# A grouped expert feed-forward kernel: the first block of each expert at a fixed address, and work moved between engines and queues

## The reference

```
h = gelu(einsum('bsh,bhi->bsi', x, Wi[expert]) + bi[expert])     # (32, 64, 1024)
o = einsum('bsi,bih->bsh', h, Wo[expert]) + bo[expert]
r = o + x
y = (r - mean(r)) * rsqrt(var(r) + 1e-12)
out = y * gamma[expert] + beta[expert]                            # (32, 64, 256), float32
```

## Time and profile before

| | |
|---|---|
| median of 3 runs | 142.51 us (141.81 to 144.18) |
| profiled execution, its own time | 141.87 us |
| its span, first to last instruction | 140.1 us |
| mean granted TensorE clock | 0.963 of full |
| DMA traffic | 29.78 MB, mean 212 GB/s |
| blocks of 4 samples | 9 |

### The profile page before, as it was taken

How to read it: one execution, slowest core, us unless ns; L and a number is a source line. 1 busy time by engine, 2 the same in 40 slices (tenths; PEclk the granted TensorE clock), 3 DMA queues, 4 the chain that set the end, 5 groups by cost and what they waited for, 6 DMA issues and landing times.

```text
span 140.1 us, 2511 instructions
## 1 busy us (share of the span) xinstructions
PE 116.3 (83%) x838; PEld 109.3 (78%) x838; DVE 100.0 (71%) x202; ACT 73.2 (52%) x135; POOL 74.4 (53%) x84
## 2 busy tenths in 40 slices
PE   0599901999899989989998998999899979978800
PEld 0498701999799979979997997999799879968700
DVE  3300079257978997897899799889979958676650
ACT  4002397377466738756673876576387743550000
POOL 3050270402767666576857658586839845543460
PEclk9999995599999999999999999999999999999995
DMA  4899988993199559919954991796380230101111
GB/s 107 308 290 393 395 276 315 411 392 122 37 328 402 178 147 391 396 40 306 373 221 136 389 401 57 264 384 256 80 336 4 62 104 0 37 7 42 37 37 37
DMA packets 11009, 29.78 MB, mean 212 GB/s; under 512 B 1644, under 2 KB 6252, under 8 KB 8812
## 3 DMA queue, kind: packets, MB, share of 16 engines
q1 hardware_dynamic: 8540, 22.59, 43.1%
q0 software_dynamic: 1728, 4.72, 10.6%
q10 hardware_dynamic: 720, 2.23, 4.8%
HBM read 27.17 MB, written 2.36 MB: 211 GB/s over the span
## 4 chain that ended last, share of the span: by engine, by line
PE 34%; DVE 27%; ACT 14%; issue 12%; DMA 8%; SPq 1%; POOLq 1%; POOL 1%; DVEq 0%; ACTq 0%
PE preact L618 7%; DMA wi_in<-w_in 6%; ACT wi_hi L381 6%; PE preact L592 6%; PE preact L591 6%; PE sums_ps L642 4%; DVE h_lo L508 4%; PE sums_ps L591 4%; PE sums_ps L592 4%; DVE wi_lo L484 4%; ACT h_hi L410 4%; DVE xT_r L501 4%; ACT preact L401 4%; DVE stats L517 3%; PE sums_ps L639 2%
## 5 line engine op out<-in xcount | busy, mean ns | idle before, releaser
L618 PE MATMUL preact<-xT_r,wi_lo 128*128 128x256 f32 x128 | 38.9, 304 | 9.7 <-DVE xT_r L501 9.7
L401 ACT ACTIVATE preact<-preact,params 128x256 f32<-128x256 f32 x54 | 22.0, 445 | 40.5 <-PE preact L592 29.5
L591 PE MATMUL preact<-xT_r,wi_hi 128*128 128x256 f32 x128 | 36.5, 285 | 0.0
L592 PE MATMUL preact<-xT_r,wi_hi 128*128 128x256 f32 x128 | 36.4, 284 | 0.0
L508 DVE TENSOR_TENSOR h_lo<-preact,h_hi 128x512 fp32r<-128x512 f32 x27 | 18.6, 690 | 24.0 <-ACT h_hi L410 23.3
L618 PEld LDWEIGHTS preact<-xT_r,wi_lo 128*128 128x128 f32 x128 | 24.6, 193 | 13.1 <-DVE xT_r L501 12.9
L642 PE MATMUL sums_ps<-wo_r,h_lo 128*128 128x256 f32 x108 | 31.0, 287 | 1.9 <-issue 1.2
L591 PE MATMUL sums_ps<-wo_r,h_hi 128*128 128x256 f32 x108 | 30.7, 284 | 0.0
L592 PE MATMUL sums_ps<-wo_r,h_hi 128*128 128x256 f32 x108 | 30.5, 282 | 0.0
L233 POOL DMA_INDIRECT y_rows<-xs,row_of x18 | 25.0, 1388 | 9.8 <-DVE xs L530 7.2
L329 POOL TENSOR_TENSOR rstd<-var_eps,minus_half 128x1 f32<-128x1 f32 x18 | 13.1, 727 | 28.7 <-DVE var_eps L521 28.7
(11 more groups left out here) (55 smaller groups left out, 130.0 us busy)
## 6 DMA issues: line engine op xcount, KB each, us to landing
wi_in<-w_in SPq DMA_DIRECT2D x8, 1024.0 KB, 7.1
wo_in<-w_out SPq DMA_DIRECT2D x8, 1024.0 KB, 5.9
params<-vectors SPq DMA_DIRECT2D x9, 388.0 KB, 7.2
xT_in<-x_columns SPq DMA_DIRECT2D x34, 64.0 KB
wi_in<-w_in ACTq DMA_DIRECT2D x2, 512.0 KB, 5.4
wo_in<-w_out ACTq DMA_DIRECT2D x1, 1024.0 KB, 9.2
xs<-x_rows,row_of POOLq DMA_INDIRECT x18, 4.4
y_rows<-xs,row_of POOLq DMA_INDIRECT x18, 5.2
```

The costliest lines, as they stand in the source:

```text
L401: done = nc.scalar.activation(to, pre, ACT.Gelu, bias=params[:, t % PAR_RING, 3 * H + c:3 * H + c + 1])
L591: nc.tensor.matmul(columns, weight, parts[:, 0, :], start=False, stop=False)
L592: return nc.tensor.matmul(columns, weight, parts[:, 1, :], start=False, stop=stop)
L618: nc.tensor.matmul(columns, wi_lo[:, t % 2, c, k, :], xT_r[:, t % 2, k, 0, :], start=(k == 0), stop=False)
```

## The change

**Blocks.** Blocks 0 to 7 now belong to experts 0 to 7, whatever the draw: block `e` has the first four samples of expert `e` (empty rows if there are fewer, also when there are none). Only later fours of an expert are placed by the sort, from block 8 on. `MIN_BLOCKS` stays 8, `MAX_BLOCKS` goes from 14 to 15. With the draw above both kernels run 9 blocks, 3 to 8 of them in another order of experts. The samples of blocks 0 to 7 no longer need the count of the other experts' blocks, so they leave the sort after one matmul; the rest of the table follows. `expert(eng, t)` is a constant for `t < 8`.

**Loads at the start.** Block 1's `wi_in` is issued by ACT right behind block 0's `xT_in` and ahead of `wo_in` of block 0. SP issues `xT_in` of block 1, then its `params` and `wo_in`, without waiting for `table_ready`. `wi_in` has 3 slots, `params` 4.

**Engines.** The high part of `xT_r` goes from DVE (`split_x`) to ACT (`x_high`); DVE keeps the low part (`x_low`) and does it earlier in the iteration. Adding epsilon goes from DVE to GpSimd, ahead of the root. The stores go from GpSimd (one indirect transfer of 128 rows for half a block) to SP (two direct transfers of one sample each, 64 rows); the very last sample is stored by ACT. Six warm-up matmuls run on TensorE before the sort's first matmul and three behind the second, none next to block 0.

```diff
 def load_wi(eng, t, e):
-    if t == 2:
+    if t == WI_RING:
         eng.wait_ge(preact_ready, BANKS)
-    elif t > 2:
-        eng.wait_ge(wi_lo_done, wi_count(t - 2, 1))
+    elif t > WI_RING:
+        eng.wait_ge(wi_lo_done, wi_count(t - WI_RING, 1))
...
-def store(pool, t, tile):
-    pool.wait_ge(y_ready, 2 * t + tile + 1)
-    pool.indirect_dma_start(out.rearrange("o s h -> (o s) h"), rows_of(t, tile), xs[:, t % X_RING, tile, :],
-                            None).then_inc(stored[t % X_RING], 16)
+def store(eng, t, tile, first=0, count=2):
+    rows = samples(eng, t, 2 * tile + first, count)
+    eng.wait_ge(y_ready, 2 * t + tile + 1)
+    for j, b in enumerate(rows, 2 * tile + first):
+        eng.dma_start(out[bass.ds(b, 1), :, :].rearrange("o s h -> (o s) h"), slot(t, j)).then_inc(
+            stored[t % X_RING], 16)
...
 # SyncE
     load_xT(sp, 0, 0, 2)
-    sp.wait_ge(table_ready, 1)
-    second = expert(sp, 1)
-    load_wi(sp, 1, second)
     load_xT(sp, 1)
-    load_params(sp, 1, second)
-    load_wo(sp, 1, second)
+    load_params(sp, 1, 1)
+    load_wo(sp, 1, 1)
     def iteration(t, ahead):
         if ahead:
             e = expert(sp, t + 2)
             load_xT(sp, t + 2)
             load_wi(sp, t + 2, e)
             load_params(sp, t + 2, e)
+        if t >= 2:
+            store(sp, t - 2, 1)
+        if t >= 1:
+            store(sp, t - 1, 0)
+        if ahead:
             load_wo(sp, t + 2, e)
 # GpSimd
 def root(t, tile):
-    pool.wait_ge(var_ready, 2 * t + tile + 1)
+    at = 2 * t + tile + 1
+    pool.wait_ge(mean_done, at)
+    nc.gpsimd.tensor_scalar(var_eps[:, tile:tile + 1], meanvar[:, tile, 1:2], LN_EPS, None, ALU.add).then_inc(
+        var_ready, 1)
+    pool.wait_ge(var_ready, at)
     nc.gpsimd.tensor_tensor(rstd[:, tile:tile + 1], var_eps[:, tile:tile + 1], minus_half[:, :], ...
...
 # ScalarE
     load_xT(act, 0, 2, 2)
+    load_wi(act, 1, 1)
     load_wo(act, 0, 0)
...
+def x_high(t):
+    act.wait_ge(xT_loaded[t % 2], 4 * loads_of(t, 2))
+    if t >= 3:
+        act.wait_ge(preact_ready, BANKS * (t - 2) + BANKS)
+    nc.scalar.activation(x_part(t, 0), x_got(t), ACT.Copy).then_inc(x_hi_done, 1)
...
     h_high(t, 0)
+    if has_next:
+        x_high(t + 1)
     gelu(t, 1)
 # TensorE, start
+    pe.wait_ge(fills_done, 2)
+    warm_up(WARM_UP)
     pe.wait_ge(sort_step, 3)
+    nc.tensor.matmul(tab_ps[0:1, 0:FIRST], one, placed[:, 0:FIRST], start=True, stop=True).then_inc(permuted, 1)
...
-    for _ in range(WARM_UP):
-        nc.tensor.matmul(preact[:, 0, 0:P], warm[:, :], warm[:, :], start=True, stop=True)
```

More of the change, by code:

```diff
@@ L174, in expert @@
         def expert(eng, t):
-            return nc.values_load(table[0:1, T_EXPERT + t:T_EXPERT + t + 1], engines=[eng.engine], min_val=0, max_val=E - 1,
+            if t < E:
+                return t
+            at = T_EXPERT + t - E
+            return nc.values_load(table[0:1, at:at + 1], engines=[eng.engine], min_val=0, max_val=E - 1,
                                   skip_runtime_bounds_check_because="the sort places experts 0 to E - 1")
@@ L179, in row, with x_got, x_part @@
             return params[:, t % PAR_RING, which * H:(which + 1) * H]
+        def x_got(t):
+            return xT_in[:, t % 2, :, :, :].rearrange("p j k s -> p k j s")
+        def x_part(t, part):
+            return xT_r[:, t % 2, :, part, :].rearrange("p k (j s) -> p k j s", j=QUAD)
         def slot(t, j):
@@ L343, in iteration @@
                 if t >= 1:
-                    store(pool, t - 1, 0)
+                    root(t - 1, 0)
             def end(t):
@@ L449, in _ @@
             dve.wait_ge(idx_loaded, 16)
             chain(nc.vector.tensor_copy(key[:, :], idx_i[:, :]))
-            dve.wait_ge(const_step, 3)
-            chain(nc.vector.scalar_tensor_tensor(same[:, :], key[:, 0:ALL], key[:, ALL:ALL + 1], before[:, :],
-                                                 ALU.is_equal, ALU.mult, accum_out=rank[:, :]))
+            own = key[:, B:B + 1]
+            dve.wait_ge(const_step, 4)
+            nc.vector.scalar_tensor_tensor(same[:, :], key[:, 0:B], own, before[:, :], ALU.is_equal, ALU.mult,
+                                           accum_out=rank[:, :])
@@ L462, in _ @@
-            dve.wait_ge(const_step, 6)
-            chain(nc.vector.scalar_tensor_tensor(placed[:, :], slot_iota[:, :], slot_of[0:B, 0:1], sample_less[:, :],
-                                                 ALU.is_equal, ALU.mult))
+            chain(nc.vector.tensor_scalar(after[:, :], key[:, 0:B], own, None, ALU.is_gt))
+            dve.wait_ge(permuted, 1)
+            nc.vector.tensor_tensor(table[:, 0:FIRST], tab_ps[0:1, 0:FIRST], table_base[:, 0:FIRST], ALU.add).then_inc(
+                samples_ready, 1)
```

225 lines of the change are left out of this document (116 added, 109 removed).

## The result

The changed kernel takes 134.69 us (median of 4, 134.53 to 135.04) where the kernel before takes 142.91 in the same comparison: 0.945 of the time, 95% interval 0.939 to 0.952. It is faster, as forecast, but by 5.5% and not by 10%: the forecast was 128.5 and its range ended at 133.5. Timed again later it took 133.58 (133.14 to 134.55), 0.935 [0.932, 0.939]. So medians of one kernel differ by about 1 us between comparisons, and the miss is 5 to 6 us. The medians are of all executions, while the ratios leave out those that fell in a slower state of the chip (some 2 to 3 us longer), and e4 and e5, which kept too few others, have no ratio.

The account below looks back on a forecast made before the run. Between blocks DVE's written order was taken as the bound, TensorE behind it. 140.1 - 5.7 - 5.6 - 0.8 - 1.9 = 126.1 us of span, 128.5 as the median; range 125.5 to 133.5.

Parts of the forecast that it names:

- waits between blocks: TensorE's wait for xT_r at the start of iterations goes as a whole: 7 x 0.82 = 5.7 us, bounds 0 and 5.9.
- start: Block 1's weights land at 13.4, so quarter 1 of its first product begins at 22.6 instead of 28.25: 5.6 us.
- last blocks: In iteration 8 DVE reaches the branch ahead of wo_lo earlier against TensorE's time: 0.8 us, bounds 0 and 0.94.
- tail: Last finish to the end takes 2.4 us with a direct store, less 0.2 for epsilon: 1.9 us gained, bounds -0.6 and 2.8.
- block 0 runs from 8.4 to 15.6: At the start, block 0 on TensorE runs 1.6 us earlier than before, its x landing at about 8.2.
- I count 2.4 GHz throughout: TensorE keeps full clock through the start's idle times; a fall would cost up to 1.6 us.
- The sentence under which the forecast called itself wrong: Wrong if weight loads idle on another engine inside a period, or the granted clock is 0.5 around 22 us.
- (b): Rival: another wait keeps the period between blocks at 12.4, so 5.7 are not gained: 134.2; chance 0.11.
- Rival (a): At the start, block 1's weights come no earlier, landing near 15.8, and the clock falls again: 132.5; chance 0.16.
- a packet in turn from each queue: At the start, DMA engines alternate packets between queues with work; by equal turns block 1's weights land at 13.5.
- the move of the stores: Stores on SP delay no load that was early: cost nothing in the period, cover 2.1 us.
- X's place in VectorE's order: DVE makes x's low part behind h_low(t, 0), near 6.3 us into the iteration; TensorE wants it at 11.59.

Follow-up runs that it names:

- e4: Changed kernel with the second half of wo_lo made at the end of DVE's iteration, ahead of the branch, instead of at the next one's start: 134.52 us.
- e5: Changed kernel with eleven products of the warm-up tile on TensorE between the first product of block 1's first quarter and block 0's second product: 134.34 us.
- e1: Changed kernel with eight warm-up matmuls added right ahead of block 0: 133.73 us.
- e2: Changed kernel with block 2's first weights and parameters issued by SyncE right behind block 1's second weights, ahead of block 2's x: 133.95 us.
- c1: Changed kernel with the edits of e1, e2, e4 and e5 together and the epsilon back on VectorE: 130.65 us, 0.919.
- u_store_gpsimd: Changed kernel with the stores back on GpSimd, one indirect transfer for a tile, the epsilon staying on GpSimd: 138.91 us, 0.978.
- e3: Changed kernel with two of block 1's four x loads moved to ScalarE's queue, ahead of block 1's first weights: 134.76 us.
- u_eps_vector: Changed kernel with the epsilon added on VectorE again, GpSimd keeping only the root: 132.79 us, 0.937.

## Why the prediction was wrong in size

Direction and the step between blocks were right, the sum was 6.8 us short of the span (126.1 against 132.9):

| term | forecast | measured | 
|---|---|---|
| waits between blocks | 5.7 | 5.4 (0.8 ahead of T, 3.7 in five periods, 0.85 at the start of the last iteration with two products) |
| start | 5.6 | 1.3 (T 2.1 earlier, less that 0.8) |
| last blocks | 0.8 | -0.5 (-0.3, and -0.2 for the wait behind TensorE's branch, 1.73 instead of 1.57) |
| tail | 1.9 | 1.0 (last `r` to the end, 7.23 and 6.26) |

The measured terms are read from TensorE's marks and add up to the span's 7.2 within rounding.

**The start is the step that failed.** I followed block 1's weights from 13.4 on through ACT and DVE, and that number was good (13.73). At the place where my sum ended, quarter 1 of block 1's first product, most of the gain was there: 24.22, where it was 28.25 and I had 22.6, so 4.0 of 5.6 us. What is missing ahead of it is 1.1 us in which ScalarE waited for x of block 1, whose landing I never priced, and 0.3 of the weights. One iteration later, at T, 1.3 us were left. Three things in the same paragraph were wrong. First, "block 0 runs from 8.4 to 15.6". It began at 9.19, since the list of experts was read at 3.38 instead of 2.54. And its duration of 7.23 was taken from a profile in which warm-up matmuls ran until block 0's began:

```profile
6.42 3.78 PE L585 MATMUL preact<-warm 128*128 128x128 f32 x16
9.99 0.76 PE L615 MATMUL preact<-xT_in,wi_in 128*128 128x256 f32 x2
```

Now TensorE idles 1.93 us ahead of block 0 and runs its first matmuls at half rate (11 in the 5 us from 9 to 14); with the warm-up back in that place (e1) the 32 take 7.07. Second, I stopped at the second product of block 0 and never asked what is late next. It is block 2's weights, behind block 0's end in SyncE's order; they are used at 27.67, which was 27.55 before the change, and TensorE then stands 1.05 us at 37. e2 shows that they are late because they are issued late, and e5 that they are the last bound in this execution; in the second profile they are not. Third, "I count 2.4 GHz throughout", with a fall priced at up to 1.6 us and left out of the sum. The granted clock did fall, to 0.56 to 0.59 between 24 and 28 us, and TensorE took 4.41 us from quarter 1 to quarter 2 of block 1 instead of 2.91: 1.5 us, near the 1.6 priced. Its price in the kernel's time is 1.3 us where it is the bound (e2 against c1) and nothing where the weights are (e5 against the first profile). The 1.5 and the stall of 1.05 are nearly all of the 2.7 us that were lost between that place and T. The sentence under which the forecast called itself wrong, a granted clock near 0.5 after the idle time, came true 2 to 3 us later than it said.

None of the rivals was right. The number of (b), 134.2, is nearest to 134.69, and that is luck: its mechanism, a period that stays at 12.4, is refuted by 11.65. Rival (a), 132.5, had the term right, a start that gains little. But block 1's weights did come earlier, so its mechanism is false; and undoing their early issue costs nothing, as the rule of the Trainium skill cited there (DMA: Bandwidth & Descriptors, Issuing engines are not separate DMA queues) would have it. The other rule cited, a packet in turn from each queue, the trace bears out in part. Between 12 and 13 us both queues moved 48 packets, and between 13 and 14 ScalarE's moved 42 and SyncE's 43:

```profile
q10 hardware_dynamic: 48, 0.39, 92.7%
q1 hardware_dynamic: 48, 0.02, 8.0%
...
q10 hardware_dynamic: 42, 0.33, 77.4%
q1 hardware_dynamic: 43, 0.02, 7.1%
```

I used it for the weights (13.5, nearly right) and not for the queue beside them. Equal packets are unequal bytes: SyncE's x of block 1 goes in small packets, gets 0.02 MB in that microsecond, and was waited for until 16.4. That isn't the whole cause: from 9 to 11 us ScalarE's queue moved 100 packets and SyncE's 5, though the last of x was issued by 9.3, and from 11 to 12 it was 56 to 146. Why SyncE's queue moved so little before 11 the profile doesn't say.

**Between blocks** the wait went as a whole and nothing took its place, as forecast. The period fell by 0.76 (0.74 on TensorE) and not 0.82. The reason given was incomplete, though. I priced the move of the stores at nothing in the period; u_store_gpsimd shows that beside the new epsilon on GpSimd they are worth 0.70 a block on TensorE's marks (0.85 on VectorE's), more than x's move (0.58 and 0.60). Both engines feed the same VectorE iteration: x's parts lie in it, and it waits for the root. The two don't add: 0.70 and 0.58 are more than the 0.74 of the change, and undone alone they take back 5.3 and 5.7 us (5.1 without its slowest execution) of the 9.0 that the change gives in that comparison, by the medians. That the stores bounded the period of the kernel before isn't shown, as VectorE hardly waited for a root there (1.6 us in all). X's place in VectorE's order, which the forecast named first, is worth 0.14 of it.

**Last blocks.** Right that a branch makes VectorE late, wrong that it would be absorbed. TensorE now comes to it without the 0.83 us wait that it had just ahead, so the stall of 1.58 meets it earlier, and it waits 1.21. The expected 0.8 was the old wait moved, not removed. e4 shows that it could be removed: with `wo_lo` ahead of the branch the wait is gone and 1.3 us with it.

**Tail.** Two sizes. The direct store ends 3.3 us after the last finish (forecast 2.4; the indirect one 4.54), so that the move gains 1.2 and not 2.1. And the epsilon costs 0.2 to 0.3 at the end (forecast 0.2), which leaves 1.0 of 1.9. I had priced the store by a 4 KB load; the 64 KB transfer lands 2.0 us after its issue in the median (page), and it is issued 0.2 us after `finish`; what fills the last microsecond to the end the profile doesn't say.

## What to carry over

When a start is to be shortened, follow the chain until the loop is in its rhythm, not to the first wait that goes: here three bounds (weights, x, clock) stood within 2 us of each other, which of them came last changed between two executions of one kernel, and taking one alone gave nothing that could be told from the scatter. A duration measured on TensorE just after a warm-up isn't valid where the change puts an idle time ahead of it. And when an engine's iteration is shortened from two sides to get below another's, price each side with the other in place as well: here each, undone alone, took back nearly the whole step.

## What the runs showed of the hardware

- The granted clock in the windows isn't enough to tell TensorE's rate at a program's start: from 9 to 14 us it says 1.00 while 11 matmuls run in 5 us (some 0.45 us each, against 0.23 in the kernel before, 32 in 7.23 us). In e3, with the same 7 matmuls from 9 to 12, it says 0.50.
- A GpSimd operation on 128x1 takes 0.51 us in the changed kernel (18 times, mean 511 ns on the page), and 0.15 on VectorE. The power takes 0.72 alone (kernel before, u_eps_vector). In the changed kernel, right behind the epsilon, it takes 0.56 to 0.57 in 12 of 18 cases and 1.40 to 1.46 in the other 6, 0.86 in the mean; why wasn't tried.
- The list of experts is read at 3.21 to 3.66 us in all thirteen profiles of the changed kernel and its variants, and was at 2.54 in that of the kernel before, though the load is issued at the same time (0.79 and 0.80) and a little smaller. It takes back most of what the shorter table gave. Its cause wasn't tried.
- The idle time behind a branch out of the nested `If`s was between 1.20 and 2.04 us on TensorE ahead of the last block's second product, in thirteen profiles, and it varies from one execution of a kernel to the next (1.73 and 1.20).
